# Six score banks read in pairs, one bank for the other products, and two activations on VectorE

## The reference

```python
def layer(h, p):                       # 6 layers, h is 8 x 512 x 128, H = 16 heads of DH = 8
    q = (h @ wq.T + bq_).reshape(bh, sl, H, DH)
    k = (h @ wk.T + bk_).reshape(bh, sl, H, DH)
    scores = jnp.einsum('blhd,bmhd->bhlm', q, k) * inv_sqrt_d
    w_avg = jax.nn.softmax(scores, axis=-1).mean(axis=1)
    new_w = jax.nn.softmax(CSCALE * w_avg + rel[None], axis=-1)
    sa = jnp.einsum('blm,bme->ble', new_w, h)
    h1 = _ln(h + sa, l1w, l1b)
    h2 = _ln(h1, l2w, l2b)
    ff = jax.nn.relu(h2 @ w1.T + b1_) @ w2.T + b2_
    return (_ln(h2 + ff, l3w, l3b), None)
...
x = x + attn(_layernorm(x))            # the 6 layers
x = x + ffn(_layernorm(x))             # silu gate, two 512x512 gelu layers, one projection
```

## Time and profile before

| what | value |
|---|---|
| median of 3 runs | 2704.5 us (2704.07 to 2704.79) |
| profiled execution | 2701.24 us, span 2699.4 us |
| PE busy | 2533.7 us, 94% |
| DVE busy | 2452.7 us, 91% |
| ACT busy | 2437.3 us, 90% |
| POOL busy | 1432.4 us, 53% |
| mean granted TensorE clock | 0.994 |

### The profile page before, as it was taken

One profiled execution on the slowest core, in us unless ns is written; L12 is line 12 of the kernel. 1 busy time (PEld: TensorE's weight loads), 2 busy tenths in 40 slices (PEclk: granted clock), 3 DMA queues, 4 the chain that ended last, 5 costly groups with the idle time before them and its releaser, 6 DMA issues.

```text
span 2699.4 us, 88896 instructions
## 1 busy us (share of the span) xinstructions
PE 2533.7 (94%) x35336; PEld 1213.7 (45%) x35336; DVE 2452.7 (91%) x5616; ACT 2437.3 (90%) x6799; POOL 1432.4 (53%) x1564
## 2 busy tenths in 40 slices
PE   6899999999999999999999999999999999988999
PEld 1344444444444444444444444444444443446777
DVE  6999999999999999999999999999999999963333
ACT  5999999999999999999999999999999999972222
POOL 3567765565555655655656556555566555544000
PEclk8999999999999999999999999999999999999999
DMA  4222212211122112121121122111211211100000
GB/s 130 66 67 72 81 60 65 68 53 56 54 69 64 48 50 68 53 72 54 53 64 46 52 84 69 55 55 53 64 60 53 69 44 55 50 14 17 16 16 24
DMA packets 98913, 152.86 MB, mean 57 GB/s; under 512 B 17857, under 2 KB 81089, under 8 KB 88897
## 3 DMA queue, kind: packets, MB, share of 16 engines
q1 hardware_dynamic: 97936, 146.26, 17.4%
q10 hardware_dynamic: 560, 0.92, 0.1%
HBM read 92.58 MB, written 41.94 MB: 50 GB/s over the span
## 4 chain that ended last, share of the span: by engine, by line
ACT 35%; DVE 35%; PE 19%; issue 9%; POOL 0%; SPq 0%; DMA 0%; POOLq 0%; ACTq 0%; DVEq 0%
ACT ex L883 31%; DVE negmax L706 25%; PE m L1022 4%; PE mean L1110 3%; PE sc L1110 3%; PE mean L1033 3%; DVE pt L717 2%; PE sc L1015 2%; DVE bn L667 2%; ACT ew L889 2%; ACT relu L934 1%; DVE mv L658 1%; DVE veps L662 1%; PE m L1041 1%; PE m L1122 1%
## 5 line engine op out<-in xcount | busy, mean ns | idle before, releaser
L883 ACT ACTIVATE ex<-sc,negmax 128x512 f32<-128x512 f32 x3072 | 2131.2, 824 | 21.7 <-DVE negmax L706 19.9
L706 DVE TENSOR_REDUCE negmax<-sc 128x1 f32<-128x512 f32 x3072 | 1926.2, 676 | 37.3 <-PE sc L1015 22.8
L1015 PE MATMUL sc<-kb,qb 96*32 96x512 bf16 x12288 | 1060.4, 385 | 107.1 <-ACT ex L883 91.1
L883 ACT ACTIVATION_READ_ACCUMULATOR ex<-sc,negmax 128x1 f32 x3072 | 1058.6, 345 | 0.0
L1033 PE MATMUL mean<-ex,rw 128*32 128x512 f32 x6144 | 803.3, 593 | 7.5 <-ACT ew L889 7.5
L1015 PEld LDWEIGHTS sc<-kb,qb 96*32 96x32 bf16 x12288 | 331.6, 94 | 978.8 <-ACT ex L883 826.9
L525 POOL TENSOR_TENSOR rw<-sel_sb,zinv 128x256 f32<-128x256 f32 x384 | 236.0, 615 | 616.8 <-DVE zinv L712 616.7
L1033 PEld LDWEIGHTS mean<-ex,rw 128*32 128x32 f32 x6144 | 199.4, 110 | 157.0 <-issue 80.0
L1022 PE MATMUL m<-hc,pt 128*32 128x129 f32 x6144 | 205.9, 274 | 6.7 <-DVE pt L717 3.5
L1022 PE MATMUL m<-h2t,w_sb 128*32 128x512 f32 x1536 | 204.8, 597 | 5.4 <-ACT relu L934 2.7
L497 POOL TENSOR_TENSOR rstd<-veps,nhalf 128x4 f32<-128x4 f32 x160 | 163.0, 1019 | 78.1 <-DVE veps L664 54.7
(11 more groups left out here) (111 smaller groups left out, 2450.1 us busy)
## 6 DMA issues: line engine op xcount, KB each, us to landing
kb<-qk_split SPq DMA_DIRECT2D x288, 128.0 KB
qb<-qk_split SPq DMA_DIRECT2D x568, 64.0 KB
qk_split<-kp SPq DMA_DIRECT2D x144, 128.0 KB, 1.8
qk_split<-qp SPq DMA_DIRECT2D x141, 128.0 KB, 1.8
hc<-hs SPq DMA_DIRECT2D x48, 256.0 KB, 2.7
xin<-x SPq DMA_DIRECT2D x16, 256.0 KB, 2.7
fh_raw<-fh SPq DMA_DIRECT2D x2, 1024.0 KB, 5.2
y_kept<-xin SPq DMA_DIRECT2D x8, 256.0 KB, 2.0
```

The source lines that it names most:

```text
L706: nc.vector.tensor_reduce(negmax[:, s % RT:s % RT + 1], sc[s % NS][:, :], AX, ALU.max, negate=True) \
L883: nc.scalar.activation(ex[:, s % ET, :], sc[s % NS][:, :], ACT.Exp, bias=negmax[:, c:c + 1], accum_out=zsum[:, c:c + 1]).then_inc(exp_read ...
L1015: ins = nc.tensor.matmul(sc[s % NS][h * QS:h * QS + QS, :], qb[t % 2][:, h % 2, g, h // 2, r:r + QS], kb[t % 2][:, g, h // 2, :], start=Tr ...
```

## The change: pairs, one bank less, and work moved between engines

The score banks become one tensor of six (NS = 6). VectorE takes the maximum of two neighbouring banks in one instruction, at every second tile; ScalarE's exponentials wait for the number of such instructions (`reductions`). The bank `m0` goes: its transposes, attention products and their readers use `m1`, and `m1_read` waits for the readers of both. The copy `h3t` and the keys `kf` of all but the first inputs move from ScalarE to VectorE. The sums `veps` and the product `zz` move from VectorE to GpSimd, as five operations of 128x4 a unit, and centring waits for the aggregates rather than for `veps`. The whole table STEP has new numbers.

```diff
-NS = 5
+NS = 6
-    "sum_heads": (21, 22, 25, 26, 32, 34, 45, 47, 52, 57, 61, 64, 69, 72, 73, 75),
+    "sum_heads": (19, 23, 28, 29, 34, 36, 45, 48, 51, 57, 61, 65, 71, 71, 76, 77),
-    "up": (146, 151, 156, 158),
-    "relu": (146, 150, 153, 158),
+    "up": (155, 156, 157, 161),
+    "relu": (151, 153, 155, 157),
...
+MAX_AT = (2, 0, 2, 0, 2, 0)
+def reductions(s):
+    return s // 2 + 1
...
+        sc_all = ctx.enter_context(nc.psum_tensor("sc", [P, NS, S], f32))
+        sc = [sc_all[:, i, :] for i in range(NS)]
-        m0 = ctx.enter_context(nc.psum_tensor("m0", [P, S], f32))
...
             def power(k, n):
+                if k == 0:
+                    gp.wait_ge(res_ready, n * NT)
+                    nc.gpsimd.tensor_tensor(ze[:, :], res[:, :, E], eps4[:, :], ALU.mult).then_inc(ze_ready, 1)
+                    gp.wait_ge(ze_ready, n)
+                    nc.gpsimd.tensor_tensor(zz[:, :], ze[:, :], res[:, :, E], ALU.mult).then_inc(zz_ready, 1)
+                    gp.wait_ge(zz_ready, n)
+                gp.wait_ge(mv_ready[k], n)
+                nc.gpsimd.tensor_tensor(veps[:, k, :], mv[:, k, :, 1], (eps if k else zz)[:, :], ALU.add).then_inc(veps_ready[k], 1)
...
+            def keys_late(n):
+                dve.wait_ge(k_ready, n + 1)
+                dve.wait_ge(k_part, 4 * n)
+                nc.vector.tensor_scalar(kf[:, :], m1[:, :], bqk_sb[LAYER_OF[n] % 2][:, 1:2], 1.0, ALU.add, ALU.mult) \
+                    .then_inc(kf_ready, 1)
...
             def score_max(t, j):
                 s = t * TILES + j
-                dve.wait_ge(scores_ready, s + 1)
-                nc.vector.tensor_reduce(negmax[:, s % RT:s % RT + 1], sc[s % NS][:, :], AX, ALU.max, negate=True) \
-                    .then_inc(max_ready, 1)
+                n = MAX_AT[s % NS]
+                if n:
+                    dve.wait_ge(scores_ready, s + n)
+                    nc.vector.tensor_reduce(negmax[:, s % RT:s % RT + n], sc_all[:, s % NS:s % NS + n, :], AX, ALU.max, negate=True) \
+                        .then_inc(max_ready, 1)
...
+                for t in due("norm3_out", 0, g, j):
+                    dve.wait_ge(xh3t_ready, late_input(t) + 1)
+                    nc.vector.tensor_copy(h3t[:, :], m1[:, :]).then_inc(ht_ready, 1)
...
-            def m0_read():
-                once("qf", qf_ready, PRE)
-                once("pt", pt_ready, put["turned"])
-                once("res", res_ready, put["attended"])
...
+                once("pt", pt_ready, put["turned"])
+                once("res", res_ready, put["attended"])
```

More of the change, by code:

```diff
@@ L77 @@
[L77 to L107, removed]
@@ new lines @@
+    "stats0": (42, 84, 86, 86),
+    "spread": (87, 107, 177),
+    "power": (92, 114, 178),
+    "apply0": (99, 102),
+    "norm1_weight": (102,),
+    "norm1_bias": (102,),
+    "stats1": (99, 102, 102, 104),
+    "apply1": (113, 146),
+    "norm2_turn": (151,),
+    "norm2_out": (149,),
+    "token_weight": (150,),
+    "token_bias": (157,),
+    "up": (155, 156, 157, 161),
+    "relu": (151, 153, 155, 157),
+    "down": (168, 170, 171, 171),
+    "add": (171,),
+    "stats2": (173, 174, 175, 175),
@@ new lines @@
+    "apply2": (182, 186),
+    "norm3_turn": (191,),
+    "norm3_out": (191,),
+    "norm3_weight": (188,),
+    "norm3_bias": (189,),
+    "project": (193, 203),
+    "queries": (193,),
+    "keys": (202,),
+    "split_q": (219, 233, 238, 239),
+    "split_k": (218, 219, 233, 236),
+    "last_weight": (190,),
+    "last_bias": (191,),
+    "last_add": (203,),
+    "last_stats": (196,),
+    "last_spread": (199,),
+    "last_power": (209,),
+    "last_apply": (209,),
+    "last_turn": (208,),
+    "last_keep": (205,),
@@ new lines @@
+    "first_stats": (0, 3, 27, 27),
+    "first_spread": (34,),
+    "first_power": (42,),
+    "first_apply": (45, 47),
+    "first_turn": (49,),
+    "first_out": (45,),
+    "first_token": (70,),
+    "first_project": (51, 58),
+    "first_queries": (50,),
+    "first_keys": (55,),
+    "first_split_q": (65, 66, 66, 71),
+    "first_split_k": (71, 72, 73, 74),
+    "head_high": (1, 4, 6, 13, 35, 37, 41, 66),
+    "head_low": (14, 28, 34, 37, 45, 61, 81, 81),
+    "head_first": (66, 72, 73, 81, 83, 96, 98, 107),
@@ L659, in spread @@
                 ins.then_inc(mv_ready[k], 1)
-                dve.wait_ge(mv_ready[k], n)
-                if plus is None:
-                    nc.vector.tensor_scalar(veps[:, k, :], mv[:, k, :, 1], EPS, None, ALU.add).then_inc(veps_ready[k], 1)
-                else:
-                    nc.vector.tensor_tensor(veps[:, k, :], mv[:, k, :, 1], plus, ALU.add).then_inc(veps_ready[k], 1)
             def stats(src, k, i):
@@ L819, in _ @@
                     queries(late_input(t))
+                for t in due("keys", 0, g, j):
+                    keys_late(late_input(t))
                 for i in range(NT):
@@ L871, in _ @@
             first_copy(1)
-            act.wait_ge(filled, 5)
+            act.wait_ge(filled, 7)
             act.wait_ge(q_kept, 48)
@@ L878, in exp_scores @@
                 s = t * TILES + j
-                act.wait_ge(max_ready, s + 1)
+                act.wait_ge(max_ready, reductions(s))
                 if s >= ET and s % 4 == 0:
@@ L935, in _ @@
                                              bias=col[RUN[t] % 2][:, C_B1 + c:C_B1 + c + 1]).then_inc(relu_ready, 1)
-                for t in due("norm3_out", 0, g, j):
-                    act.wait_ge(xh3t_ready, late_input(t) + 1)
-                    nc.scalar.activation(h3t[:, :], m1[:, :], ACT.Copy).then_inc(ht_ready, 1)
-                for t in due("keys", 0, g, j):
-                    keys(late_input(t))
                 for b in due("first_out", 0, g, j):
@@ L975, in _ @@
                 pe.wait_ge(first_ready, b + 1)
-                wait_later(pe, ht_ready, b)
+                wait_later(pe, qf_ready, b)
                 transpose_tokens(xin[b], xh3t_ready)
                 pe.wait_ge(ht_ready, b + 1)
-                wait_later(pe, qf_ready, b)
-                nc.tensor.matmul(m0[:, :], wqk_sb[0][:, 0, :], h3t[:, :], start=True, stop=True).then_inc(q_ready, 1)
+                nc.tensor.matmul(m1[:, :], wqk_sb[0][:, 0, :], h3t[:, :], start=True, stop=True).then_inc(q_ready, 1)
                 wait_later(pe, kf_ready, b)
```

110 lines of the change are left out of this document (47 added, 63 removed).

## The result

The changed kernel takes 2698.41 us (median of 11 runs, 2695.64 to 2701.58), the kernel before 2704.07 us beside it: ratio 0.9977, 95% interval 0.9968 to 0.9987. Forecast was 2677. The two profiled executions are 2698.99 and 2701.24 us, so their traces explain 2.25 us of a difference of 5.7: the profiled execution of before is 3 us shorter than its median, and a window of one profile can be off by as much.

What follows compares the result with a forecast made beforehand. ScalarE and VectorE, both nearly full, were taken to bound the units and TensorE the tail. At 48.45 us a unit, forty units gave -24, the last eight -3 and the tail 0: 2677 us, range 2648 to 2714.

Steps and rivals of the forecast that it cites:

- my case: Whole kernel: the forecast's main account, a gain of 10 to 42 us, at a chance of 0.45.
- Pair maximum 1.13: VectorE's maximum over two score banks: 1.13 us from start to start, against 2 x 0.60 for two singles.
- Demand of ScalarE 47.15: ScalarE's work per unit once copy and keys have left it: 47.15 us, down from 48.2.
- Stand of 0.7 to 1.0 before slot 44: Slots 34 to 44: VectorE's lead of 1.0 us runs out, so ScalarE stands idle 0.7 to 1.0 us.
- 0.5 us from slot 50 to 24: Slot 50 to 24 of the next unit: loads level in sum, but copy and keys find no lead; 0.5 us of stands.
- The sum of 48.45: A middle unit: ScalarE's 47.15 plus stands of 0.8 and 0.5 gives 48.45 us, 0.6 less than before.
- From 24 to 34 VectorE ... must wait for banks: Slots 24 to 34: VectorE has 5.8 us of work against ScalarE's 8.8, so its spare is spent waiting.
- Forty units give -24: The forty units that have copy and keys: 0.6 us saved in each, 24 us together.
- In the last eight ... I take -0.4 x 8: Last eight units, without copy and keys: only VectorE is relieved, taken as a gain of 3 us.
- Tail 0 (-5 to +5): After the units: stays TensorE-bound, so the reordered squares were counted as 0, within -5 to +5 us.
- Rival C: TensorE stopped at slot 34's head sum by GpSimd's row weights, or by m1's handovers: 2700 to 2725 us, chance 0.16.
- Rival A: Whole kernel: ScalarE alone is the bound, its stands shrinking to 0.3 to 0.7 us a unit: 2635 to 2655 us, chance 0.25.

Runs made afterwards that it cites:

- e14: The changed kernel with single maxima in slots 44 and 45 alone, pairs elsewhere; 2708.16 us, ratio 1.0015.
- e7: The changed kernel with each unit's add two slots later (171 to 173) and its statistics at 174 to 175; 2724.0 us, ratio 1.0081.
- e12: The changed kernel with the unit's last down at 173, the add at 174, and its statistics, aggregates and power later; 2748.6 us, ratio 1.0169.
- e3: The changed kernel with single maxima in slots 24 to 37 of each unit, pairs elsewhere; 2724.0 us, ratio 1.0081.
- e6: The kernel before with zz and veps on GpSimd, aggregates not waiting for their own result, copy and keys on VectorE; 2707.07 us, ratio 1.0008.
- e4: The changed kernel with the copy h3t and the keys back on ScalarE; 2743.86 us, ratio 1.0151.
- e9: The changed kernel's table and engine moves with before's five single score banks, single maxima and two product banks; 2917.2 us, ratio 1.0788.
- e1: The kernel before with only the changed kernel's table rows for head_square, head_gelu and head_split; 2696.88 us, ratio 0.998.
- e10: The kernel before with zz and veps on GpSimd, aggregates not waiting for their own result, and the changed kernel's order of squares; 2688.2 us, ratio 0.994.

## Why the prediction was wrong in size

The time lies above my case's own range (2662 to 2694), and its gain of 5.7 us is about the 5.4 that I had called no change, at a chance of 0.08. The account had the span 27 us shorter, the traces have it 2.2 shorter. Of the 24 to 25 us between them 13 lie in units 6 to 38, 8 in units 0 to 5 and nearly 11 in units 39 to 47; 7.8 came back after the last exponential, where I had counted nothing.

- **Pair maximum 1.13:** right, 1.132. The Trainium skill (Perfetto Trace Analysis, Optimizing Scalar/DVE Operations) states about 125 ns of overhead for VectorE on PSUM; the pair saves 2 x 0.60 - 1.132 = 0.07, so the trace disagrees with that size.
- **Demand of ScalarE 47.15:** nearly right; 64 x 0.663 + 4 x 0.477 + 5 x 0.57 = 47.2.
- **Stand of 0.7 to 1.0 before slot 44:** right, 0.91, though the sum took 0.8, and there for the reason given, VectorE's work in that stretch. That it is not the pair's length, e14 shows. Two things the forecast had not seen: TensorE is nearly as late there (e7, e12), and the stretch begins at the attend's handover and not with the lead at slot 34 (e3).
- **0.5 us from slot 50 to 24:** near, 0.44 in the pieces listed.
- **The sum of 48.45:** this failed by its size. The stands were 1.7 and not 1.3: 0.1 more before 44, and about 0.3 spread over slots in pieces too small to list, for which the account had no term. So 48.91 a unit; in units 6 to 38 -6.6 us and not -20.
- **"From 24 to 34 VectorE ... must wait for banks":** it waits 2.6 us there, but in unit 20 the waits of 0.86 and 0.93 stand behind `up` products that wait 0.63 each for a relu.
- **"Forty units give -24":** this failed. The account was made for a middle unit and multiplied. In the first six VectorE carries the first layer's steps too, and 298.5 us stand against 293.9, +4.6 where -3.6 was counted. e6 shows for before's banks that the moved copy and keys are paid in full there; in the changed kernel the same move gains in those units (e4 52.4, changed 51.2), so its surcharge comes from pairs, banks and table, and which of them is open. The single bank is not it alone: e9, with two, has 55.8 there against 53.7 in the middle.
- **"In the last eight ... I take -0.4 x 8":** this failed too, by sign: +1.0 a unit in 44 to 46. I took VectorE's relief for a gain. Without ScalarE's relief the rest of the change costs 0.9 (e4).
- **Tail 0 (-5 to +5):** -7.8, of which the squares' order makes 4.9 (e1, which gains 5.7 us in all). Less that, by subtraction, the change is no gain; that it comes out faster at all is owed to a term that I had put at nothing.
- **Rival C:** its first place was wrong. The weights for the sum of slot 36 end at 1038.4 in unit 20 and the next head sum starts at 1041.08; GpSimd's five small operations take 0.20 each. Its second, the handovers of m1, was real (84.3 us of waits for relu against 49.4), and I had priced them at nothing in my own case; how much of it reaches ScalarE, no run shows. The two banks are written 17 times a unit, not 16.
- **Rival A** needed stands of 0.3 to 0.7; they are 1.7 (48.91 - 47.2).

In one line: the terms of demand were right, the stands grew from 0.9 to 1.7 in a middle unit and not to 1.3, and in the first and last units they grew by more. The small gain of the middle was undone, and more, by units that the account had covered only by multiplying; what is left of the gain lies in the tail.

## What to carry to other kernels

Follow each kind of unit by itself, the first and the last layer above all; a gain worked out for the middle one was a loss in a dozen others. An engine with about 3 us of waits a unit can still be the bound: look for the stretch between a handover of fixed place and its next wait, for there added work was paid in full (0.60 us in e3, 0.07 in e14), and moving the add within it (e7) or splitting a pair (e14) gained nothing. Before taking a many-part change as a whole, run its parts: here two of them on the old banks (e10) gave 0.6% where all together gave 0.23%.
